# A gated attention and routed-expert block on one core: the first two gathered expert tiles moved into the last steps of the row-tile loop, and the leftover logits and transposes moved between their products

## The reference: what is computed

```python
# attention weights only; the "values" are not multiplied: the probabilities (512 x 512) are the result
probs = softmax(where(mask, -inf, (ctx @ Wq.T + bq) @ (ctx @ Wk.T + bk).T * 128**-0.5 * layernorm(x)))
x = x + tanh(g_xattn) * probs
h = layernorm(x)
# router: 8 experts, the 2 best of sigmoid(h @ Wg.T) + bias, weights normalised over the two
# expert e: silu(h @ W1[e].T) * (h @ W3[e].T) * weight[e]  ->  @ W2[e].T ; 256 hidden features
x = x + tanh(g_ffn) * sum over the two chosen experts
```

## Time and profile before

| | us |
|---|---|
| median of 3 runs | 326.88 (326.1 to 329.94) |
| profiled execution, its own time | 325.86 |
| its span in the profile | 323.9 |
| PE busy | 279.9 (86%) |
| POOL busy | 196.5 (61%) |
| DVE busy | 191.4 (59%) |
| ACT busy | 127.3 (39%) |
| mean granted TensorE clock | 0.919 of full speed |

### The profile page before, as it was taken

The page is one execution under the profiler, slowest core; times in us unless marked ns, Lnnn a source line. Parts: engine busy times, 40 slices in busy tenths (PEclk is TensorE's granted clock), DMA queues, the critical chain, the costliest instruction groups (busy, mean ns, idle before and its releaser), DMA issues.

```text
span 323.9 us, 5197 instructions
## 1 busy us (share of the span) xinstructions
PE 279.9 (86%) x1316; PEld 203.7 (63%) x1316; DVE 191.4 (59%) x505; ACT 127.3 (39%) x239; POOL 196.5 (61%) x208
## 2 busy tenths in 40 slices
PE   3699799487997696988999996999999999999980
PEld 1145364253354584866888775888888888888860
DVE  2698777899598977598345425444535445454530
ACT  2678569133566652222233222333332332333220
POOL 5188897618777777557776448465646445653313
PEclk9979989655599679999999999999999999999997
DMA  7999898783353361546464657666767556766435
GB/s 230 317 397 328 270 329 301 255 301 138 127 170 133 92 192 34 100 69 101 93 121 76 97 99 112 111 117 110 143 95 124 108 83 115 134 126 97 46 54 65
DMA packets 27026, 48.69 MB, mean 150 GB/s; under 512 B 9524, under 2 KB 10296, under 8 KB 25976
## 3 DMA queue, kind: packets, MB, share of 16 engines
q0 software_dynamic: 9760, 20.49, 36.1%
q1 hardware_dynamic: 14408, 15.04, 14.5%
q10 hardware_dynamic: 2832, 12.85, 11.7%
HBM read 28.51 MB, written 19.85 MB: 149 GB/s over the span
## 4 chain that ended last, share of the span: by engine, by line
DMA 45%; issue 19%; POOL 11%; PE 10%; DVE 9%; ACT 3%; POOLq 2%; SPq 1%; ACTq 0%; DVEq 0%
DMA out<-rows,slot 30%; DMA out<-rows 10%; POOL out L460 4%; POOL rows L441 4%; PE bank L902 2%; DMA rows<-in_x 2%; POOL slot_table L428 2%; POOLq L452 2%; DVE w_lo L841 1%; DMA w_hi<-in_ctx_t 1%; DVE rows L698 1%; DMA rows<-xn_rows,slot 1%; DVE w_hi L675 1%; PE bank L909 1%; PE bank L981 1%
## 5 line engine op out<-in xcount | busy, mean ns | idle before, releaser
L460 POOL DMA_INDIRECT out<-rows,slot x39 | 62.3, 1598 | 65.4 <-DMA out<-rows,slot 42.1
L993 PE MATMUL bank<-w_hi,xt_hi 128*128 x156 | 64.7, 414 | 0.0
L994 PE MATMUL bank<-w_lo,xt_hi 128*128 x156 | 61.1, 392 | 0.0
L995 PE MATMUL bank<-w_hi,xt_lo 128*128 x156 | 61.0, 391 | 0.0
L820 DVE TENSOR_TENSOR xt_lo<-bank,xt_hi 128x512 fp32r<-128x512 f32 x39 | 26.9, 690 | 50.7 <-ACT xt_hi L584 50.7
L592 ACT ACTIVATE rows<-bank 128x256 f32<-128x256 f32 x39 | 15.0, 384 | 88.1 <-PE bank L995 88.1
L441 POOL DMA_INDIRECT rows<-xn_rows,slot x39 | 39.2, 1005 | 16.2 <-issue 10.2
L605 ACT ACTIVATE rows<-bank,slot 128x512 f32<-128x512 f32 x39 | 26.8, 687 | 50.0 <-PE bank L1022 39.0
L428 POOL DMA_INDIRECT slot_table<-entry,slot_index x32 | 33.1, 1034 | 17.8 <-DVE slot_index L783 9.0
L826 DVE SCALAR_TENSOR_TENSOR rows<-rows,bank 128x256 f32<-128x256 f32 x39 | 16.4, 420 | 38.7 <-ACT rows L592 38.5
L1020 PE MATMUL bank<-w_hi,gt_hi 128*128 x78 | 30.9, 396 | 4.8 <-DVE gt_lo L837 4.8
(11 more groups left out here) (131 smaller groups left out, 454.6 us busy)
## 6 DMA issues: line engine op xcount, KB each, us to landing
w_lo<-in_w ACTq DMA_DIRECT2D x8, 1024.0 KB, 7.6
xn_rows<-w_hi SPq DMA_DIRECT2D x17, 256.0 KB, 6.8
rows<-in_x SPq DMA_DIRECT2D x16, 256.0 KB, 4.3
out<-rows SPq DMA_DIRECT2D x16, 256.0 KB, 3.9
w_lo<-in_w ACTq DMA_DIRECT2D x8, 512.0 KB, 4.5
w_hi<-in_ctx_t SPq DMA_DIRECT2D x4, 256.0 KB, 5.3
slot<-slot_table SPq DMA_DIRECT2D x39, 1.0 KB, 2.2
rows<-xn_rows,slot POOLq DMA_INDIRECT x39, 4.3
```

The lines of the kernel that those rows point to most:

```text
L460: pool.indirect_dma_start(out=out[0:SPARE + P * READY[segment(i)], :], out_offset=bass.IndirectOffsetOnAxis(ap=slot[:, i, 0:1].bitcast(U32 ...
L993: pe.matmul(ps_h[i % 2][:], xt_hi[:, i % 2, k, :], hi, start=(k == 0), stop=False)
L994: pe.matmul(ps_h[i % 2][:], xt_hi[:, i % 2, k, :], lo, start=False, stop=False)
L995: mm = pe.matmul(ps_h[i % 2][:], xt_lo[:, i % 2, k, :], hi, start=False, stop=(k == KC - 1))
```

## The change: what it does

- **x's finished rows are stored by ACT** (`store_x1` moves from SP's to ACT's program, after `squares`), on the queue that carries the weight loads. One weight load of each early step moves a step later.
- **Routing of the first group a step earlier.** positions(0) is at the end of PE's step 8 instead of in step 9, router_slots(0) follows router_weights(0) in DVE's step 8; the 14 scatters go in steps 8 to 11 instead of 9 to 12. SP reads slots 0 to 2 in step 13 and 3 to 6 in step 14, ahead of later stores of normed rows.
- **Projections.** PE makes q and k of the next sequence in step 2, 6, 10 ahead of logits and transpose and in place of the spin; ACT copies them out in step 3, 7, 11 after the exponential. Spins write another bank.
- **Splits.** SPLITS has 23 units in the 16 steps (22 before), with two units a step in steps 8 to 11, 13 and 14. Unit 19 moves from step 14 to step 13, and it overwrites the buffer of the even normed rows, so it waits for the store of normed row 12.
- **Gathers.** gather(0), gather(1) are in POOL's step 14, gather(2) follows the loop, and gather(3) follows normed(15). normed(14) and normed(15) write in place, so each waits until its finished row is stored.
- **PE.** After the loop: gathered(0), gathered(1), hidden(0), then logits(13), transpose(14), gathered(2), hidden(1), gate_transpose(0), logits(14), transpose(15), gathered(3), output(0), gate_transpose(1), logits(15), positions(1), hidden(2). hidden(0) no longer waits for squares.
- **ACT.** gathered_hi(0) and gathered_hi(1) are in step 15 right after exponentials(15), ahead of transposed(13), unit 22 and squares(15).
- **Second group's routing.** router_weights(1), router_slots(1), list_tiles(1) are in DVE's turns 0, 1 and 2 of the second phase; its 8 scatters are in POOL's turns 0 and 1, ahead of add_rows(0). The third group's routing is one turn later.

```diff
-    SPLITS = (1, 1, 2, 2, 1, 2, 1, 2, 1, 1, 1, 2, 1, 1, 2, 1)
-    LO_BY_POOL = (0, 1, 2, 4, 6, 7, 9, 10)
-    LOADS = {0: (2,), 1: (3,), 2: (4,), 4: (5,), 5: (6,), 6: (7,), 7: (8,), 8: (9, 10, 11), 9: (12,), 10: (13,), 11: (14,),
-             12: (15,)}
-    SCATTERS = {9: (0, 0, 3), 10: (0, 3, 6), 11: (0, 6, 10), 12: (0, 10, 14)}
-    LATE_SCATTERS = {0: (1, 6, 8), 4: (2, 0, 2), 5: (2, 2, 3), 6: (2, 3, 5), 7: (2, 5, 6), 8: (2, 6, 8), 9: (2, 8, 9),
-                     10: (2, 9, 10)}
+    SPLITS = (1, 1, 1, 1, 1, 2, 1, 1, 2, 2, 2, 2, 1, 2, 2, 1)
+    LO_BY_POOL = (0, 1, 2, 3, 4, 6, 7, 9)
+    LOADS = {1: (2,), 2: (3,), 4: (4,), 5: (5,), 6: (6,), 7: (7,), 8: (8, 9), 9: (10, 11), 10: (12,), 11: (13,), 12: (14,),
+             13: (15,)}
+    SCATTERS = {8: (0, 0, 3), 9: (0, 3, 7), 10: (0, 7, 11), 11: (0, 11, 14)}
+    LATE_SCATTERS = {0: (1, 0, 6), 1: (1, 6, 8), 5: (2, 0, 2), 6: (2, 2, 4), 7: (2, 4, 5), 8: (2, 5, 7), 9: (2, 7, 8),
+                     10: (2, 8, 10)}
...
-        ps_h = bank[0:2]
+        ps_h = (bank[5], bank[0])
...
-        ps_o = (bank[5], bank[3])
+        ps_o = (bank[1], bank[3])
...
+        def prob(tile):
+            return x_row(TILES - 4) if tile >= TILES - 2 else prob_sb
+
         def normed_row(tile):
-            if tile == TILES - 1:
-                return x_row(TILES - 3)
-            return early(15, 1) if tile % 2 == 0 else early(13, 1)
+            if tile >= TILES - 2:
+                return x_row(tile)
+            return xn_even if tile % 2 == 0 else xn_odd
...
-                if step == TILES - 1:
+                if step == TILES - 3:
                     listed(0)
-                    for i in range(4):
+                    for i in range(3):
                         load_slots(i)
-                if 1 <= step <= TILES:
-                    store_x1(step - 1)
+                elif step == TILES - 2:
+                    for i in range(3, FIRST[1]):
+                        load_slots(i)
...
             def normed(tile):
-                if tile == TILES - 1:
-                    row_done(TILES - 3)
+                if tile >= TILES - 2:
+                    pool.wait_ge(s_x1_out[tile % XR], 16 * (tile // XR + 1))
...
-            gather(0)
-            gather(1)
+                if step == TILES - 2:
+                    gather(0)
+                    gather(1)
+            gather(2)
             row_scales(TILES)
             normed(TILES - 1)
-            gather(2)
             gather(3)
-            enter_slots(1, 0, 6)
...
             def transposed(tile):
...
-                if tile == TILES - 1:
-                    row_done(TILES - 2)
+                if tile >= TILES - 2:
+                    act.wait_ge(s_xn_out[tile % 2], 16 * (tile // 2 + 1))
...
                 if unit == 2 * E + 3:
+                    act.wait_ge(s_exp, TILES - 2)
+                    act.wait_ge(s_xpose, TILES - 3)
+                    act.wait_ge(s_xn_out[0], 16 * (TILES // 2 - 1))
...
                 exponentials(step)
+                if step % NT == 3 and step // NT + 1 < B:
+                    project(step // NT + 1)
+                if step == TILES - 1:
+                    gathered_hi(0)
+                    gathered_hi(1)
                 if step >= 2:
                     transposed(step - 2)
-                for unit in units_in(step)[0:2]:
-                    if unit != 2 * E + 4:
-                        split_hi(unit)
+                for unit in units_in(step):
+                    split_hi(unit)
...
                 squares(step)
-                if step == TILES - 2:
-                    split_hi(2 * E + 4)
-                if step % NT == 2 and step // NT + 1 < B:
-                    project(step // NT + 1)
+                store_x1(step)
...
                 hidden_tanh(i)
+                if i == 0:
+                    split_hi(UNITS - 1)
+                    transposed(TILES - 2)
+                elif i == 1:
+                    transposed(TILES - 1)
...
             for i in range(LIST):
                 gate_rows(i)
+                if i == 0:
+                    split_lo(UNITS - 1)
                 if i + 2 < LIST:
                     gathered_lo(i + 2)
                 gated_transposed(i)
                 if i == 0:
+                    router_weights(1)
+                elif i == 1:
+                    router_slots(1)
+                elif i == 2:
                     list_tiles(1)
...
                 if i == 0:
-                    logits(TILES - 1)
+                    logits(TILES - 3)
+                    transpose(TILES - 2)
                     gathered(2)
                 elif i == 1:
                     gate_transpose(0)
+                    logits(TILES - 2)
+                    transpose(TILES - 1)
                     gathered(3)
                     output(0, last)
                     gate_transpose(1)
+                    logits(TILES - 1)
+                    positions(1)
```

More of the change, by code:

```diff
@@ L90, in flamingo_routed_block @@
         xg = rows[:, 0:XG]
-        y = rows[:, XG:XG + 2]
-        gate = rows[:, XG + 2].rearrange("p (r s) -> p r s", r=2)
+        gate = rows[:, XG].rearrange("p (r s) -> p r s", r=2)
+        y = rows[:, XG + 1:XG + 3]
         xt_hi = sb("xt_hi", [P, 2, KC, P], F32R)
@@ L114, in flamingo_routed_block @@
         attn_neg = early(10, 2).bitcast(BF16).rearrange("p (t s) -> p t s", t=NT)
-        prob = early(14, 1)
+        q_sb = early(12, 1)
+        k_sb = early(13, 1)
+        xt_sb = early(14, 1)
+        xn_odd = early(15, 1)
         bqk_sb = sb("bqk_sb", [P, 2])
@@ L438, in gather @@
                     pool.wait_ge(s_x, i - XG + 1)
+                elif i == XG - 1:
+                    pool.wait_ge(s_exp, TILES)
                 else:
@@ L531, in exponentials @@
                 act.wait_ge(s_nb, tile + 1)
-                act.activation(ps_s[tile % 2][:], prob, ACT.Exp, bias=nbias[:, t:t + 1],
+                act.activation(ps_s[tile % 2][:], prob(tile), ACT.Exp, bias=nbias[:, t:t + 1],
                                scale=rstds[:, t, 0:1], accum_out=prob_sum[:, t:t + 1]).then_inc(s_exp, 1)
@@ L539, in squares, with store_x1 @@
                                accum_out=sqsum2[:, t:t + 1]).then_inc(s_sq, 1)
+            def store_x1(tile):
+                act.wait_ge(s_x1, tile + 1)
+                act.dma_start(out[SPARE + tile * P:SPARE + (tile + 1) * P, :], x_row(tile)).then_inc(s_x1_out[tile % XR], 16)
             def transposed(tile):
@@ L674, in scores @@
                 dve.wait_ge(s_scores, tile + 1)
-                dve.scalar_tensor_tensor(out=prob, in0=x_row(tile), scalar=mv1[:, t, 0:1],
+                if tile == TILES - 2:
+                    dve.wait_ge(s_xn, TILES - 3)
+                    dve.wait_ge(s_x1_out[(TILES - 4) % XR], 16 * ((TILES - 4) // XR + 1))
+                dve.scalar_tensor_tensor(out=prob(tile), in0=x_row(tile), scalar=mv1[:, t, 0:1],
                                          in1=ps_s[tile % 2][:], op0=ALU.subtract, op1=ALU.mult).then_inc(s_z, 1)
@@ L678, in scores @@
                 dve.wait_ge(s_neg, tile + 1)
-                dve.tensor_tensor_reduce(prob, prob, ps_neg[:], 1.0, LOWEST, ALU.add,
+                dve.tensor_tensor_reduce(prob(tile), prob(tile), ps_neg[:], 1.0, LOWEST, ALU.add,
                                          ALU.max, zmax[:, t:t + 1]).then_inc(s_zmax, 1)
@@ L869, in _ @@
                     router_weights(0)
+                    router_slots(0)
                 elif step == END[0] + 2:
-                    router_slots(0)
                     list_tiles(0)
+            gathered_lo(0)
+            gathered_lo(1)
+            for unit in units_in(TILES - 1):
+                split_lo(unit)
             router_ranks(1)
-            router_weights(1)
-            gathered_lo(0)
-            router_slots(1)
-            gathered_lo(1)
-            for unit in range(2 * E + 5, UNITS):
-                split_lo(unit)
             for i in range(LIST):
                 gate_rows(i)
+                if i == 0:
+                    split_lo(UNITS - 1)
                 if i + 2 < LIST:
@@ L1037, in _ @@
                     masks(step + 1)
-                if step == END[0] + 2:
-                    positions(0)
-                if step < TILES - 2:
-                    spin(projected)
-                if step >= 2:
-                    logits(step - 2)
-                if step >= 1:
-                    transpose(step - 1)
                 if step % NT == 2 and step // NT + 1 < B:
                     project(step // NT + 1)
-                    projected += 1
-            logits(TILES - 2)
+                elif step < TILES - 2:
+                    spin(step)
+                if 2 <= step < TILES - 1:
+                    logits(step - 2)
+                if 1 <= step < TILES - 1:
+                    transpose(step - 1)
+                if step == END[0] + 1:
+                    positions(0)
             gathered(0)
-            positions(1)
```

(1 more changed line is left out.)

72 lines of the change are left out of this document (28 added, 44 removed).

## The result

The changed kernel takes 337.72 us (median; 335.43 to 341.31) against 327.01 for the kernel before beside it: a ratio of 1.0288 (1.0167 to 1.041): slower, though the interval leaves open whether by more than 2%. The profiled execution took 335.7 with a span of 333.7 (before 325.86 and 323.9), at a mean granted clock of 0.924 (0.919). Forecast 332.2, range 325 to 340: the sign and the range were right, and so was the place, the second group's late slots. The size was too small: 6.4 us more were foretold, and the profiled execution took 9.8 more, the medians 10.7. Executions of one kernel differ by 1 to 3%, and a profile shows only one of them, which can be a short or a long one.

The account below looks back on a forecast made before the run. Adds following each other by their landings, not PE, were taken as the clock from 131.68 to about 203 us. Terms of -4.4, +9.2 and +1.6 gave +6.4 on 325.86: 332.2 us, range 325 to 340.

Parts of the forecast that it names:

- E: End of residual(15), where the second group's ranks begin: 109.16 us before the change, foretold 104.8 after it.
- Rival 1: PE, not the adds, sets the end: 318.2 us, if add_rows(0) goes out no later than 131.7; chance 0.13.
- Rival 3: Losses are smaller: unit 19 waits little and PE is at full clock, 2.0 us back each: 328.2; chance 0.20.
- Rival 4: Something holds the gathers in POOL's step 14, hidden(0) begins no earlier, second group later still: 341 us; chance 0.05.
- (a): Steps 3 to 7, row stores on ACT: 23.7 us instead of 28.5, a gain of 4.8 (bounds 0 and 5.3).
- S8: DVE's scores(8), S with a number being scores of that step; near 47.6 us was a sign for (a).
- rival 2: Row stores stay slow behind the weight loads, so (a) gives 0 and the rest stands: 337.0 us; chance 0.24.
- (b): Steps 8 and 9, 22.4 us before: a gain of 1.6, with 0.6 lost to a second cast ahead of router's tanh.
- (d): Step 13 to E: 17.7 us instead of 14.4, as unit 19's cast waits for normed row 12's store; loss 3.3.
- S9: DVE's scores(9), the start of its step 9, when POOL's scatters were taken to begin.
- (g): First add to gather(15), 55.6 us before: one scatter more in turns 5 and 10, a loss of 1.6 (0 to 2.5).
- (e): E to the second group's first scatter: 20.1 us after E instead of 8.7, including 2.0 for PE's lower clock.

Follow-up runs that it names:

- e1: The changed kernel with the second group's ranks, weights and slots made right after gathered_lo(1), and positions(1) right after hidden(0): 331.59 us, ratio 1.0242.
- c2: c1 with the edits of e2 and e3 added: 327.64 us, ratio 0.9988 to the kernel before.
- d4: c2 with third group's routing one turn earlier, first gathers after POOL's loop, second group's slots and positions ahead of the gathered tiles: 327.17 us, ratio 0.9999.
- e4: The changed kernel with only the finished rows' stores moved back from ACT's to SP's program: 339.22 us, ratio 1.0456.
- e2: The changed kernel with only unit 19's split moved back from ACT's step 13 to step 14: 337.04 us, ratio 1.0398.
- c1: e1 with the second group's list of tiles moved from DVE's turn 2 to turn 0: 335.81 us, ratio 1.024.
- e3: The changed kernel with two low splits exchanged, unit 8's to POOL and unit 9's to DVE: 332.72 us, ratio 1.0264.

## Why the prediction was right, and which terms were not

**What held.** The forecast's mechanism: late slots shift the adds, and the early products give nothing. The first scatter is E + 18.8 (20.1 foretold), scatters to add 11.6 (11.6), PE is full behind gather(15), and e1, c2 and d4 take the shift away by the order and the assignment of work alone. In all fourteen profiled executions 128.1 to 129.8 us lie between gather(15) and the end of the last product, and 5.7 to 6.9 between the end of the third group's last scatter and gather(15), while E lies anywhere from 106.1 to 118.2. What sets the time is thus the string from E through slots, adds and scatters to gather(15). That "the adds are the clock, not PE" up to 203 was too strong all the same: before the change PE was busy for 20.00 of the 20 us from 160 to 180. hidden(0) ran at half clock: 0.63 a product and 5.0 for twelve, where hidden(1) took 2.8. Rival 1 (PE sets the end) fell: add_rows(0) at 143.42 is far from the 131.7 that it needed, and d4 puts early products at about 2 us where slots are early. Rival 3 fell: unit 19's cast waited 4.08, not little, and hidden(0) was not at full clock. Rival 4 fell: the gathers left at 107.82. The forecast had given "slower" 0.44 and "within 2%" 0.43, so on that count it had hardly chosen.

**(a) Row stores.** 25.2 against 23.7, inside the bounds. The 23.7 was itself added up wrong: two steps of 4.0, one of 5.2, one of 5.1 and the 5.7 of step 3 make 24.0. And of the 8.2 us of waits for x that it was to take away only 5.4 lie in steps 3 to 7. The sign set for it did not come: S8 was 49.30, not 47.6, and two waits for x came behind step 3 (2.32 and 0.59). Such waits fell with the stores on ACT, as e4 says, but how much time that gave can't be told from what one execution differs from another. The rule set against it, in the Trainium skill, DMA: Bandwidth & Descriptors, Queues, rings and completion order, is that a ring is consumed in order. The DMA issues from 12 to 50 us, first before, then after:

```profile
w_lo<-in_w ACTq DMA_DIRECT2D x6, 1024.0 KB, 7.6
out<-rows SPq DMA_DIRECT2D x6, 256.0 KB, 5.4
...
rows<-in_x SPq DMA_DIRECT2D x5, 256.0 KB, 3.9
```
```profile
w_lo<-in_w ACTq DMA_DIRECT2D x6, 1024.0 KB, 9.0
out<-rows ACTq DMA_DIRECT2D x8, 256.0 KB, 5.3
rows<-in_x SPq DMA_DIRECT2D x7, 256.0 KB, 8.2
```

A store takes as long on ACT's ring as on SP's. The loads of x take longer to land, 8.2 for 3.9, but are issued earlier. The trace agrees with the rule: a weight load lands 9.0 after its issue, the next store is issued some 4 us behind it and lands 5.3 later, about when the load does. So rival 2's premise, that a store gets no faster, is what the row shows; that (a) then gives 0 in time is neither shown nor excluded.

**(b) Steps 8 and 9**, the first failed term: "Gain 1.6" was a loss of 1.8. I put the second cast's cost to the router's tanh at 0.6; DVE waited 1.46 for it, since PE had five filler products (1.25) ahead of the logits. 0.59 went to x. And a list instruction took 2.29 instead of 0.15.

**(d) Step 13 to E**, the mis-sized term: 17.7 foretold, 21.1 measured. The path was the one described, but "normed row 12 is ready at S9 + 32.2" came at 98.47 + 0.77, S9 + 36.2. S13 itself was 1.9 later after S9 than foretold, which (b) holds, so 2.0 of it falls here. SP then issued that row's store only at 101.10, 1.9 behind the row, where I had 0.8: its three reads of slots stood ahead. SP's timeline, then ACT's:

```profile
98.47 2.58 SPq L341 DMA_DIRECT2D slot<-slot_table  x3
101.10 0.43 SPq L329 DMA_DIRECT2D xn_rows<-w_hi  x1
```
```profile
103.31 1.04 ACT L578 CAST w_hi<-w_lo 128x1024 fp32r<-128x1024 f32 x1 [4.08 <-DMA xn_rows<-w_hi]
```

I costed POOL's scatters at 1.26 throughout, that is 0.96 and a gap of 0.30. But three that began while DVE was in a split took 1.63 to 1.99, the first one 1.26, and one instruction of row_scales 1.75 (0.72 elsewhere). Together that is 3.8 of the 4.0. The cast came at S13 + 11.3 instead of 8.3. scores(14) waited 1.62 for normed row 12 as well, but DVE stood behind the cast afterwards, so that wait set nothing.

So E, foretold 4.4 earlier with bounds of -0.4 and 7.6, was 3.9 later, outside them: (a) 1.5, (b) 3.4 and (d) 3.4 too good.

**(g)** went the other way: 54.0 for 57.2. Turn 4 lost both its scatters, and adds 2 and 3, of one expert, were 3.2 apart, where they had been 5.8. I had counted the scatters added to turns 5 and 10 and not those taken from turn 4. This and (e) hid 4.5 of the 8.3 that E was off; that the median came out near is partly their doing.

## What to carry to other kernels

When work is pulled ahead into a gap, list what it now stands in front of on each engine: here early products are worth about 2 us, and the slots queued behind them came 10 us later after the first phase's end. If a chain of accumulations paces a phase, order every engine's program by who feeds that chain first. And one profiled execution can't price an edit of the first phase here to better than 3 us or so (steps 3 to 7 alone took 24.6 to 28.3); compare distances between named instructions, with the clock of the same window.

## What the runs showed of the hardware

**DVE and POOL hold each other.** In the change's step 9 a DVE instruction on 6 numbers took 2.29 us and ended with POOL's split (72.71 and 72.70); its neighbours took 0.15 to 0.33. DVE's timeline, then POOL's:

```profile
70.06 0.33 DVE L811 TENSOR_TENSOR list_row<-compared 1x7 int32<-1x7 f32 x1
70.42 2.29 DVE L815 TENSOR_TENSOR compared<-list_expert 1x6 f32<-1x6 int32 x1
72.75 0.15 DVE L817 SCALAR_TENSOR_TENSOR list_landed<-compared,landed_base 1x6 int32<-1x6 f32 x1
```
```profile
70.35 2.35 POOL L423 TENSOR_TENSOR w_lo<-w_lo,w_hi 128x1024 fp32r<-128x1024 f32 x1
...
82.30 1.99 POOL L430 DMA_INDIRECT slot_table<-entry,slot_index  x1 [0.30 <-issue]
84.60 0.96 POOL L430 DMA_INDIRECT slot_table<-entry,slot_index  x1 [0.30 <-issue]
```

The same instruction took 2.28 or 2.29 in all five kernels in which POOL has its split in that step (the change, e1, e2, e4, c1), and 0.15 in the nine others, e3 among them. The other way round, POOL's scatter that began at 82.30, inside DVE's splits (81.11 to 83.46), took 1.99, where the next took 0.96. Of the first group's 196 scatters in the fourteen traces 23 took 1.63 or more, and all 23 began while DVE was in a low split; none of the others took over 1.31, though 17 of them began in one too. That the two engines share something is inferred from this; no run took them apart, and it is not shown why 17 passed.
